# A graph network's gates and its experts in one stage: the gates computed in four groups, three of them between the experts' units

## The chip, the cores and the metric

The program runs on one core of one Trainium2 chip. Its metric is the device time of one execution in microseconds, the median of the runs. The profile was taken in one further execution.

## What is computed

The kernel is a tower of four layers over 16384 tokens of 64 features. The change touches the feed-forward part of the third layer: a graph attention gives every node four scores, the best two of them become gates, and a mixture of four experts, computed densely, is weighted by these gates.

```python
e = jax.nn.leaky_relu(a_src[src] + a_dst[dst], negative_slope=0.2)
e_max = jax.ops.segment_max(e, dst, num_segments=M)
ee = jnp.exp(e - e_max[dst])
denom = jax.ops.segment_sum(ee, dst, num_segments=M)
alpha = ee / (denom[dst] + 1e-16)
msg = h[src] * alpha[:, :, None]
agg = jax.ops.segment_sum(msg, dst, num_segments=M).reshape(M, HEADS * NUM_EXPERTS) + b_gat
scores = _layernorm(agg, ln_gamma, ln_beta).reshape(M, HEADS, NUM_EXPERTS).mean(1)
scores = scores.reshape(Bc, Nc, NUM_EXPERTS)
topk_s, topk_i = jax.lax.top_k(scores, TOP_K)
w = jax.nn.softmax(topk_s, axis=-1)
for ei in range(NUM_EXPERTS):
    g = jnp.where(topk_i == ei, w, 0.0).sum(-1)
    hh = jax.nn.gelu(x @ W1[ei] + b1[ei], approximate=False)
    out = out + g[..., None] * (hh @ W2[ei] + b2[ei])
```

## The kernel before

The program is a row of stages. Each is a `Stage` with its own tiles and semaphores, and ends with a barrier over all engines (L82). Inside a stage each engine has its own instruction stream, written out by hand, and semaphores tie the streams together, so the order of the work is the order of the code. Tokens lie in 128 tiles of 128 (`TILES`).

The third layer's feed-forward part (`ffn2`, L3941) has these stages around the change:

- `edge_softmax` runs over all edges and leaves in DRAM, row by row (`q.t_state`), the running softmax states of the edges sorted by destination.
- `carry_states` (L3753, names `carry_`) mends the states of nodes whose edges go over the end of a partition's row. It is a chain over SP, DVE, ACT and POOL, most of it on one partition, and ends with an indirect store by POOL (L3791).
- `node_gates` (L3841, names `gates_`): POOL issues 128 indirect gathers, one a tile (L3929), each 32 of them one group with a semaphore of its own. DVE waits for a group and merges it with the node's own state (L3880 to L3902), four times, 32 tiles at a time. Then it goes on over all 128 tiles at once: normalisation (L3905 to L3908), the scores (L3910, L3911), the best two in `top2_steps` (L665 to L685), and the gates split into three bf16 parts (`GateSplit.vector`, L775 to L779). PE turns them (L788) in 8 steps of 16 tiles, and ACT copies each step from PSUM into `g.GT` (L795). POOL, behind its gathers, clears the room for the split gates and makes the experts' tables (`ExpertTables`, L832 to L839); SP loads the weights (L817 to L828).
- `experts` (L1203, names `expc_`): 16 blocks of 8 tiles times 4 experts make 64 units. PE spreads a unit's gates over the partitions (`gate`, L1289, tile `gp`) and computes the first layer of the next unit (L1271, tile `hp`); ACT applies Gelu (L1351); DVE multiplies both into `hid` (L1394); PE multiplies by the second weights (L1303), with six bias matmuls at a block's first expert (L1301). At a block's end ACT copies the sum (L1341), PE turns it back (L1312, at the third unit of the next block), DVE adds it to `g.H` (L1372, one unit later) and takes the statistics of the block before (L1377).

Two rules of that loop matter here. PE's `gate(u)` waits until product u - 1 is done, since `gp` has one buffer. And PE's stream has for unit u the order gate(u), first layer (u + 1), second layer (u - 1).

## Time and profile before

| | |
|---|---|
| median of 3 runs | 6085.68 us (6083.33 to 6087.12) |
| the profiled execution | 6076.21 us, span 6074.5 us |
| PE busy | 4905.7 us (81%), mean granted clock 0.899 |
| DVE busy | 4695.5 us (77%) |
| POOL busy | 2671.5 us (44%) |
| ACT busy | 2461.6 us (41%) |
| from the first gather of `node_gates` to the last statistics of `experts` | 4611.3 to 4998.7 us of the span |

The granted clock stands in tenths or as a share: 1.00 is PE's full clock and 0.50 the half. Start times are microseconds from the span's start. PE is the matmul engine, PEld its weight loads, DVE the vector engine, ACT the scalar engine, POOL GpSimd, SP the engine that issues DMAs. A bracket behind a timeline row gives the engine's idle time just before and what ended it.

### The profile page before, as it was taken

What the parts mean: (1) busy time and instruction counts of PE and PEld (TensorE: products, weight loads), DVE (VectorE), ACT (ScalarE), POOL (GpSimd) and SP (SyncE); (2) the same over time, 40 slices, a digit from 0 to 9 for tenths busy, and PEclk for the clock granted to TensorE, in tenths of its full rate; (3) what the DMA queues carried; (4) which work ended last, traced back from release to release, by engine and by line L of the source; (5) the groups of instructions that cost most, each with busy time, mean ns of one, the idle gap of its engine ahead of it and who ended that gap; (6) DMA issues with size and microseconds to landing.
All of it is one profiled execution on the core that took longest, in us unless ns stands there. A gap on an engine that the chain in (4) does not pass through costs nothing. (4 is left out here: it accounts for less than half of the span.)

```text
span 6074.5 us, 108916 instructions
## 1 busy us (share of the span) xinstructions
PE 4905.7 (81%) x39862; PEld 3331.9 (55%) x39929; DVE 4695.5 (77%) x8591; ACT 2461.6 (41%) x4417; POOL 2671.5 (44%) x3019
## 2 busy tenths in 40 slices
PE   5567968886637999998799999999990298967998
PEld 3463226664424666665677777777770027852452
DVE  7896988897696888887588888888883467767657
ACT  4453433333434666666233333343340143222332
POOL 0000010000324675886667777777774301015557
PEclk8787989998668999999799999999995599978999
DMA  0300000111312110000122222222220000030252
GB/s 18 84 1 6 8 23 28 30 32 39 109 50 36 19 28 17 2 2 9 28 41 43 46 44 44 43 44 43 43 44 15 5 1 4 3 74 18 67 133 44
DMA packets 269133, 208.06 MB, mean 34 GB/s; under 512 B 139498, under 2 KB 242835, under 8 KB 267571
## 3 DMA queue, kind: packets, MB, share of 16 engines
q1 hardware_dynamic: 195806, 145.14, 8.5%
q0 software_dynamic: 72912, 57.02, 6.1%
q8 instruction: 269, 4.41, 0.3%
q14 instruction: 134, 1.10, 0.1%
q10 hardware_dynamic: 12, 0.39, 0.0%
HBM read 113.55 MB, written 69.40 MB: 30 GB/s over the span
## 5 line engine op out<-in xcount | busy, mean ns | idle before, releaser
L3514 PE MATMUL edges_bank<-part_room,hot_room 128*128 128x512 f32 x6656 | 1528.8, 391 | 78.2 <-ACT XT L3537 57.5
L3514 PEld LDWEIGHTS edges_bank<-part_room,hot_room 128*128 128x128 f32 x6656 | 1249.3, 188 | 357.8 <-ACT XT L3537 69.7
L3493 POOL DMA_INDIRECT XT<-gat_node_table,edges_idx x1216 | 1203.2, 989 | 392.5 <-issue 311.8
L3537 ACT COPY XT<-edges_bank 128x512 f32<-128x512 f32 x832 | 474.8, 597 | 657.6 <-PE edges_bank L3514 562.9
L3632 DVE COPY_PREDICATED XT<-edges_tabs_p,XT 128x1024 f32<-128x1024 int32 (+7 forms) x768 | 576.9, 751 | 38.3 <-DVE edges_acc_s L3681 7.1
L3613 DVE TENSOR_SCALAR hot_room<-edges_lanes,edges_nodes 128x512 fp32r<-128x512 f16 (+1 forms) x768 | 351.1, 518 | 172.0 <-PE edges_bank L3514 86.2
L505 POOL TENSOR_TENSOR X<-H,ln_f_mean 128x1024 f32<-128x1024 f32 x5 | 11.4, 2279 | 913.2 <-DVE ln_f_shift L542 913.2
L1837 ACT ACTIVATE GT<-attc_sc,attc_nm 128x256 f32<-128x256 f32 x1024 | 399.5, 480 | 32.0 <-DVE attc_nm L1915 32.0
L1915 DVE TENSOR_REDUCE attc_nm<-attc_sc 128x4 f32<-128x1024 f32 x256 | 312.8, 1222 | 110.1 <-PE attc_sc L1756 110.1
L1851 ACT ACTIVATE GT<-attc_sct 128x1024 f32<-128x1024 f32 x256 | 262.1, 1024 | 305.3 <-PE attc_sct L1767 305.2
L1756 PE MATMUL attc_sc<-XT,attc_tT 64*128 64x256 f32 x2048 | 296.5, 409 | 43.8 <-ACT GT L1837 43.8
L1920 DVE TENSOR_REDUCE attc_rs<-GT 128x4 f32<-128x1024 f32 x256 | 309.2, 1208 | 1.8 <-ACT GT L1837 1.8
L1777 PE MATMUL attc_op<-GT,attc_xB 128*64 128x256 f32 x2048 | 278.4, 392 | 5.2
L1767 PE MATMUL attc_sct<-attc_tT,XT 64*128 64x256 f32 x2048 | 268.3, 379 | 1.3 <-DMA attc_tT<-X 0.7
L1756 PEld LDWEIGHTS attc_sc<-XT,attc_tT 64*128 64x128 f32 x2048 | 185.8, 190 | 143.3 <-issue 117.2
L2190 ACT ACTIVATE X<-attb_r 128x2048 f32<-128x2048 f32 x64 | 120.1, 1877 | 270.3 <-PE attb_r L2147 270.3
L1767 PEld LDWEIGHTS attc_sct<-attc_tT,XT 64*128 64x128 f32 x2048 | 204.8, 188 | 21.4 <-ACT GT L1851 2.2
L788 PE MATMUL gates_gt<-identb,GT 128*128 128x128 bf16 x64 | 6.6, 277 | 259.9 <-DVE GT L779 258.5
L2486 DVE TENSOR_TENSOR X<-attd_r,attd_decay 128x2048 f32<-128x2048 f32 x64 | 146.6, 2291 | 81.8 <-PE attd_r L2389 81.7
L888 POOL DMA_INDIRECT sorted_in<-X,expd_in_slot x144 | 137.9, 958 | 145.6 <-SPq L1229 88.5
L1777 PEld LDWEIGHTS attc_op<-GT,attc_xB 128*64 128x64 f32 x2048 | 129.7, 136 | 126.7 <-issue 92.7
L2234 DVE TENSOR_REDUCE attb_mx<-attb_r 128x16 f32<-128x2048 f32 x64 | 146.3, 2287 | 65.0 <-PE attb_r L2133 65.0
(850 smaller groups left out, 10203.5 us busy)
## 6 DMA issues: line engine op xcount, KB each, us to landing
gat_states<-GT SPq DMA_DIRECT2D x32, 768.0 KB, 3.3
XT<-gat_node_table,edges_idx POOLq DMA_INDIRECT x1216
edges_lanes<-gat_places SPq DMA_DIRECT2D x128, 128.0 KB, 3.0
expert_pairs<-in_L_ffn_W_dram SPq DMA_DIRECT2D x48, 256.0 KB, 4.1
edges_lanes<-gat_places SPq DMA_DIRECT2D x64, 160.0 KB, 3.2
XT<-XT SPq DMA_DIRECT2D x32, 256.0 KB
XT<-XT SPq DMA_DIRECT2D x64, 128.0 KB
XT<-XT SPq DMA_DIRECT2D x128, 64.0 KB
```

Source lines behind the costliest of these rows:

```text
L1756: m = nc.tensor.matmul(sc[(0, 1, 1, 0)[hp]][:, n, a * S:(a + 1) * S], tT[half, b % NB, hp, a * P:(a + 1) * P], x(b, half), start=True, sto ...
L1767: m = nc.tensor.matmul(sct[:, n, j * S:(j + 1) * S], x(b, half)[:, j * P:(j + 1) * P], tT[half, b % NB, hp, :], start=True, stop=True)
L1777: m = nc.tensor.matmul(op[half, 0:S], xB[:, b % NB, j, (2 * hp + n) * D:(2 * hp + n + 1) * D], probT[:, hp % 2, n, j, :], start=hp + j == ...
L1837: m = nc.scalar.activation(prob[:, hp % 2, n, a, :], sc[(0, 1, 1, 0)[hp]][:, n, a * S:(a + 1) * S], ACT.Exp, bias=nm[:, b % 2, n, hp, a:a ...
L1851: nc.scalar.activation(probT[:, hp % 2].rearrange("p n j s -> p n (j s)"), sct[:], ACT.Exp).then_inc(probT_ready, 1)
L1915: vec.tensor_reduce(nm[:, b % 2, :, hp, :], sc[(0, 1, 1, 0)[hp]][:].rearrange("p n (a s) -> p n a s", s=S), AX.X, ALU.max, negate=True).th ...
L1920: vec.reduce_sum(rs[:, b % 2, :, hp, :], prob[:, hp % 2], AX.X).then_inc(totaled, 1)
L3493: nc.gpsimd.indirect_dma_start(out=rows[:, k, c, :], out_offset=None, in_=q.t_table, in_offset=bass.IndirectOffsetOnAxis(ap=idx[:, k, c:c ...
L3514: m = nc.tensor.matmul(banks[t][:], hot[:, (k * GROUPS + j) % 2, b, t, :], parts[:, p, b].rearrange("p u c -> p (u c)"), start=b == 0 and ...
L3537: nc.scalar.copy(fetched[:, (k * GROUPS + j) % 2, t].rearrange("p u c -> p (u c)"), banks[t][:]).then_inc(fetched_in, 1)
L3613: m = vec.tensor_scalar(hot[:, (k * GROUPS + j) % 2, b, 0:GROUP_SIZES[j]], lanes[:, j % LANE_SLOTS, 0:GROUP_SIZES[j]], nodes[:, b:b + 1], ...
L3632: vec.copy_predicated(half(0, w), taken(s, w), half(w, 2 * w)).then_inc(halved, 1)
```

## The change

`node_gates` and `experts` for this layer become one stage, `merged_experts`. The gates are computed wholly by groups of 32 tiles. The first group's gates come before the first unit. A group of 32 tiles is 16 units of the experts; in what follows w is a unit's place in its group, 0 to 15. The gates of the next group are cut into pieces that DVE runs behind the products of w = 6 to 11, ACT behind its Gelus of w = 7, 8 and 10, and PE turns them at w = 12 and 13, into the PSUM tile `yt`, which serves the turn-back too. The scale is an Exp of a Ln in place of a square root and a reciprocal. The loads of the expert tables (SP), the making of `pick` and `b2f` and the clearing of the gates' room (POOL) move to `carry_states`. The small tiles of the gates lie in the unused half of `g.XT`. Nothing of the computation is left out.

```diff
-def carry_states(nc, g, q):
+def carry_states(nc, g, q, tables):
...
                 sp.dma_start(carry[:], q.t_carry).then_inc(moved, 16)
+                tables.sync(sp)
...
+                tables.gpsimd(pool)
+                nc.gpsimd.memset(g.GT[:, TOKENS // 2:].bitcast(F32), 0.0).then_inc(gates_zeroed, 1)
+                pool.wait_ge(gates_zeroed, 1)
                 pool.wait_ge(merged_ready, 1)
...
-def node_gates(nc, g, q, b_gat, gamma, beta, ahead):
...
+def merged_experts(nc, g, q, b_gat, gamma, beta, tables):
...
+    GROUPS, GT = 4, TILES // 4
+    NB = TOKENS // (2 * U)
+    NU, PER = NB * E, NB * E // 4
...
+                for t in range(TILES):
+                    nc.gpsimd.indirect_dma_start(
+                        out=run[:, t, :], out_offset=None, in_=q.t_state,
+                        in_offset=bass.IndirectOffsetOnAxis(ap=q.end_row[:, t:t + 1], axis=0)).then_inc(gathered[t // GT], 16)
...
+                def turn_gates(c):
+                    pe.wait_ge(gates_split, c // 2 + 1)
+                    if c:
+                        pe.wait_ge(gates_moved, c)
+                    if c >= 2:
+                        pe.wait_ge(y_added, NB // GROUPS * (c // 2) - 2)
+                    for k in range(8):
+                        pair = g3[:, 16 * c + 2 * k:16 * c + 2 * k + 2, :].rearrange("p t c -> p (t c)")
+                        t = nc.tensor.transpose(yt[:].bitcast(BF16)[:, k * P:(k + 1) * P], pair, g.identb[:])
+                    t.then_inc(gates_turned, 1)
...
+                    if u % PER == 0:
+                        pe.wait_ge(gates_moved, 2 * (u // PER) + 2)
+                    if u:
+                        pe.wait_ge(hid_full, u)
...
+                def turn_back(i):
+                    pe.wait_ge(y_moved, i + 1)
+                    if i:
+                        pe.wait_ge(y_added, i)
+                    if i % 4 == 2 and i + 4 < NB:
+                        pe.wait_ge(gates_moved, 2 * (i // 4) + 4)
...
+                turn_gates(0)
+                turn_gates(1)
+                for u in range(NU):
+                    gate(u)
+                    if u + 1 < NU:
+                        first_layer(u + 1)
+                    if u:
+                        out(u - 1)
+                    if u % PER in (12, 13) and u // PER + 1 < GROUPS:
+                        turn_gates(2 * (u // PER) + u % PER - 10)
+                    if u % E == 2 and u > E:
+                        turn_back(u // E - 1)
+                out(NU - 1)
+                turn_back(NB - 1)
+
+            @block.scalar
...
+                def weights(n):
+                    act.wait_ge(diff_ready, n + 1)
+                    nc.scalar.activation(diff[:, n], diff[:, n], ACT.Exp).then_inc(exped, 1)
...
+                def scales(n):
+                    mine = mean[:, n * GT:(n + 1) * GT]
+                    act.wait_ge(var_ready, n + 1)
+                    nc.scalar.activation(mine, mine, ACT.Ln, bias=g.eps[:], scale=1.0 / CH).then_inc(logged, 1)
+                    act.wait_ge(logged, n + 1)
+                    nc.scalar.activation(mine, mine, ACT.Exp, scale=-0.5).then_inc(std_ready, 1)
...
+                def gaps(n):
+                    mine = second[:, n * GT:(n + 1) * GT]
+                    act.wait_ge(gap_ready, n + 1)
+                    nc.scalar.activation(other[:, n * GT:(n + 1) * GT], mine, ACT.Exp).then_inc(gap_exped, 1)
...
+                def move_gates(c):
+                    act.wait_ge(gates_turned, c + 1)
+                    nc.scalar.copy(g.GT[:, c * 8 * P:(c + 1) * 8 * P], yt[:].bitcast(BF16)).then_inc(gates_moved, 1)
...
+                    act.wait_ge(hp_full, u + 1)
+                    if u >= 2:
+                        act.wait_ge(hid_full, u - 1)
+                    nc.scalar.activation(act_out[:, u % 2], hp[u % 2][:], ACT.Gelu, bias=b1s[:, e:e + 1]).then_inc(act_done, 1)
+                    if n + 1 < GROUPS:
+                        if w == 7:
+                            weights(n + 1)
+                        if w == 8:
+                            scales(n + 1)
+                        if w == 10:
+                            gaps(n + 1)
+                    if e == 0 and i:
+                        move_y(i - 1)
+                    if n + 1 < GROUPS and w in (13, 14):
...
+                def normed(n):
...
+                    v.wait_ge(std_ready, n + 1)
+                    link(vec.tensor_tensor(num[:, s], num[:, s], bc(mean[:, s], 2, CH), ALU.mult))
+                    link(vec.tensor_tensor(num[:, s], num[:, s], bc(params[:, 1], 1, GT), ALU.mult))
+                    link(vec.tensor_tensor(num[:, s], num[:, s], bc(params[:, 2], 1, GT), ALU.add))
+                    link(vec.reduce_sum(L[:, s], num[:, s].rearrange("p t (h e) -> p t e h", h=HEADS2), AX.X))
+                    link(vec.tensor_scalar(L[:, s], L[:, s], 1.0 / HEADS2, None, ALU.mult))
...
+                def one_hot(best, s):
+                    link(vec.tensor_reduce(best[:, s], L[:, s], AX.X, ALU.max))
+                    link(vec.tensor_tensor(hot[:, s], L[:, s], bc(best[:, s], 2, E), ALU.is_equal))
+                    link(vec.tensor_tensor(tmp[:, s], hot[:, s], bc(rev, 1, GT), ALU.mult))
+                    link(vec.tensor_reduce(r[:, s], tmp[:, s], AX.X, ALU.max))
+                    link(vec.tensor_tensor(hot[:, s], bc(rev, 1, GT), bc(r[:, s], 2, E), ALU.is_equal))
...
+                def piece(n, w):
+                    if w == 6:
+                        merge(n)
+                    if w == 7:
+                        shares(n)
+                        values(n)
+                        centre(n)
+                        spread(n)
+                    if w == 8:
+                        normed(n)
+                        best_of(n)
+                    if w == 9:
+                        second_of(n)
+                    if w == 10:
+                        mix(n)
+                    if w == 11:
+                        split(n)
...
+                for w in range(PER):
+                    piece(0, w)
+                for u in range(NU):
+                    i, e = divmod(u, E)
+                    n, w = divmod(u, PER)
+                    v.wait_ge(act_done, u + 1)
+                    v.wait_ge(gp_full, u + 1)
+                    if u >= 2:
+                        v.wait_ge(hid_used, u - 1)
+                    vec.tensor_tensor(hid[:, u % 2], act_out[:, u % 2], gp[:], ALU.mult).then_inc(hid_full, 1)
+                    if e == 3 and i:
+                        add(i - 1)
+                    if n + 1 < GROUPS:
+                        piece(n + 1, w)
+                    if e == 0 and i >= 2:
...
-            carry_states(nc, g, q)
-            node_gates(nc, g, q, I["L2_ffn_b_gat"], I["L2_ffn_ln_gamma"], I["L2_ffn_ln_beta"], ahead=tables)
-        experts(nc, g, "expc", tables, target=g.H, measure=True)
+            carry_states(nc, g, q, tables)
+            merged_experts(nc, g, q, I["L2_ffn_b_gat"], I["L2_ffn_ln_gamma"], I["L2_ffn_ln_beta"], tables)
```

DVE, around the products of w = 7 and 8 of the first group (L4169 is the product, L4039 to L4071 the merge and what follows it, L4140 the addition to `g.H`). Before, no such rows stood between products; now these do:

```order
+L4039 TENSOR_TENSOR XT<-X,XT 128x128
+L4040 TENSOR_TENSOR XT<-X,XT 128x128
+L4041 TENSOR_TENSOR XT<-XT 128x128
+L4169 TENSOR_TENSOR expc_hid<-expc_act_out,expc_gp 128x1024
+L4140 TENSOR_TENSOR H<-H,expc_yt 128x512
+L4046 TENSOR_TENSOR XT<-XT,X 128x128
+L4047 TENSOR_TENSOR XT<-XT 128x128
+L4048 TENSOR_SCALAR XT<-XT 128x128
+L4049 RECIPROCAL XT<-XT 128x128
+L4050 TENSOR_TENSOR XT<-XT 128x256
+L4057 TENSOR_TENSOR X<-X,XT 128x32x4 x4
+L4057 TENSOR_TENSOR X<-gat_table,XT 128x32x4 x4
```

The merge of the next group now stands ahead of product w = 7, and the longest piece between the products of w = 7 and 8.

ACT, from the Gelu of w = 8 to that of w = 11 (L4017 is the Gelu, L3987 the Ln, L3989 and L3994 the Exps, L4004 the copy of the block's sum):

```order
+L4017 ACT_TABLE_LOAD
+L4017 ACTIVATE expc_act_out<-expc_hp,expc_in_b 128x1024
+L3987 ACT_TABLE_LOAD
+L3987 ACTIVATE XT<-XT,eps 128x32
+L3989 ACT_TABLE_LOAD
+L3989 ACTIVATE XT<-XT 128x32
+L4004 COPY expc_yT<-expc_yp 128x512
+L4017 ACT_TABLE_LOAD
+L4017 ACTIVATE expc_act_out<-expc_hp,expc_in_b 128x1024 x2
+L3994 ACT_TABLE_LOAD
+L3994 ACTIVATE XT<-XT 128x32
+L4017 ACT_TABLE_LOAD
```

Where there was one table load in front of 64 Gelus, ACT now changes its table seven times in each of three groups.

POOL, in `carry_states` and behind it:

```order
+L3789 DMA carry_first<-gat_states,gat_first_end 128x24
 L832 MEMSET expc_in_pick 128x256
 L834 MEMSET expc_in_b2f 128x64
 L839 AFFINE_SELECT expc_in_pick<-expc_in_pick 128x512 x6
...
+L3791 MEMSET GT 128x4096
+L3795 DMA gat_states<-carry_merged,gat_first_end 262145x24
```

The tables and the clearing stood behind the 128 gathers and now stand between the two indirect DMAs of `carry_states`.

## Rows read from the trace of the kernel before

**Rows 1.** The page, part 1: busy time, share of the span and instructions of each engine.
```profile
PE 4905.7 (81%) x39862; PEld 3331.9 (55%) x39929; DVE 4695.5 (77%) x8591; ACT 2461.6 (41%) x4417; POOL 2671.5 (44%) x3019
```

**Rows 2.** Busy time by stretch: window, PE, PEld, DVE, ACT, POOL, clock, DMA share, GB/s.
```profile
4611.00:4653.00 42.00, 0.00 (x0) 0.00 (x0) 1.42 (x4) 0.00 (x0) 31.65 (x34) 0.50 0.14 20
4653.00:4774.00 121.00, 0.00 (x0) 0.00 (x0) 26.87 (x69) 1.25 (x3) 92.35 (x97) 0.50 0.10 10
4774.00:4815.00 41.00, 0.29 (x3) 0.29 (x4) 37.92 (x53) 3.69 (x5) 6.51 (x9) 0.50 0.00 0
...
4826.00:4999.00 173.00, 167.16 (x800) 49.80 (x800) 104.13 (x208) 78.70 (x81) 0.00 (x0) 0.97 0.00 1
```

**Rows 3.** Timeline, POOL (start, length, engine, line, operation, idle before).
```profile
4611.29 0.96 POOL L3929 DMA_INDIRECT X<-gat_states,gat_end_row  x1 [3.01 <-POOLq L82]
...
4771.61 0.94 POOL L3929 DMA_INDIRECT X<-gat_states,gat_end_row  x1 [0.30 <-issue]
```

**Rows 4.** Timeline, DVE, the first group's pieces.
```profile
4652.58 0.29 DVE L3880 TENSOR_TENSOR gates_m<-X,gates_own_e 128x128 f32<-128x128 f32 x1 [40.51 <-DMA X<-gat_states,gat_end_row]
...
4653.89 0.29 DVE L3885 TENSOR_TENSOR gates_den<-gates_diff,X 128x128 f32<-128x128 f32 x1 [0.48 <-ACT gates_diff L3920]
...
4656.24 0.93 DVE L3894 TENSOR_TENSOR X<-X,gates_diff 128x128 f32<-128x128 f32 x4
...
4661.90 0.69 DVE L3902 TENSOR_REDUCE gates_mean<-X 128x32 f32<-128x512 f32 x1
```

**Rows 5.** Timeline, DVE, the piece over all 128 tiles, and the first product.
```profile
4794.73 3.78 DVE L3910 TENSOR_REDUCE gates_L<-X 128x512 f32<-128x2048 f32 x1
...
4814.22 0.43 DVE L779 CAST GT<-XT 128x512 bf16<-128x512 f32 x1
...
4829.82 1.22 DVE L1394 TENSOR_TENSOR expc_hid<-expc_act_out,expc_gp 128x1024 f32<-128x1024 f32 x1 [4.00 <-ACT expc_act_out L1351]
```

**Rows 6.** Timeline, ACT, table loads and gate copies.
```profile
4775.27 1.28 ACT L3922 ACT_TABLE_LOAD   x1
...
4815.78 1.93 ACT L795 COPY GT<-gates_gt 128x1024 bf16<-128x1024 bf16 x2 [7.72 <-PE gates_gt L788]
...
4827.38 1.28 ACT L1351 ACT_TABLE_LOAD   x1 [3.56 <-PE expc_hp L1271]
```

**Rows 7.** Timeline, PE, gate matmuls at the full clock, four units apart and one apart.
```profile
4904.48 0.39 PE L1289 MATMUL expc_gp<-GT,expc_in_pick 64*128 64x512 bf16 x2
...
4912.48 0.39 PE L1289 MATMUL expc_gp<-GT,expc_in_pick 64*128 64x512 bf16 x2
...
4914.67 0.39 PE L1289 MATMUL expc_gp<-GT,expc_in_pick 64*128 64x512 bf16 x2
```

**Rows 8.** Timeline, DVE, the stage's last instructions.
```profile
4996.58 2.12 DVE L1377 BATCH_NORM_STATS2 stats<-H 128x6 f32<-128x64 f32 x16
```

**Rows 9.** Timeline, PE, one unit at the half clock, and the gate matmul of the next.
```profile
4831.10 0.61 PE L1289 MATMUL expc_gp<-GT,expc_in_pick 64*128 64x512 bf16 x2 [1.67 <-DVE expc_hid L1394]
...
4833.35 1.49 PE L1301 MATMUL expc_yp<-GT,expc_b2p 64*64 64x512 bf16 x6
4834.77 1.97 PE L1303 MATMUL expc_yp<-expc_hid,expc_in_w 128*64 128x512 f32 x4
4836.67 0.54 PE L1289 MATMUL expc_gp<-GT,expc_in_pick 64*128 64x512 bf16 x2
```

**Rows 10.** Busy time by stretch, columns as in rows 2, where the clock moves.
```profile
4824.00:4826.00 2.00, 0.03 (x2) 0.06 (x2) 1.04 (x5) 0.00 (x0) 0.00 (x0) 1.00 0.00 0
4828.00:4836.00 8.00, 6.33 (x20) 1.30 (x16) 2.44 (x2) 3.90 (x4) 0.00 (x0) 0.50 0.00 0
4836.00:4838.00 2.00, 2.00 (x9) 0.52 (x7) 0.69 (x1) 0.00 (x0) 0.00 (x0) 0.75 0.00 0
```

**Rows 11.** Timeline, DVE beside POOL's affine selects, and the selects.
```profile
4778.40 1.65 DVE L3894 TENSOR_TENSOR X<-X,gates_diff 128x128 f32<-128x128 f32 x4
...
4776.68 4.71 POOL L839 TENSOR_SCALAR_AFFINE_SELECT expc_in_pick<-expc_in_pick 128x512 bf16<-128x512 bf16 x6 [0.16 <-POOL expc_in_b2f L834]
```

More of the change, by code:

```diff
@@ new lines, in merged_experts @@
+        at = 2 * TILES * HEADS2
+        own_e, m, den = (spare[:, at + k * TILES * HEADS2:at + (k + 1) * TILES * HEADS2].rearrange("p (t h) -> p t h", h=HEADS2)
+                         for k in range(3))
+        at += 3 * TILES * HEADS2
+        L, G, hot, tmp = (spare[:, at + k * TILES * E:at + (k + 1) * TILES * E].rearrange("p (t e) -> p t e", e=E) for k in range(4))
+        at += 4 * TILES * E
+        mean, first, second, r, share, other = (spare[:, at + k * TILES:at + (k + 1) * TILES] for k in range(6))
@@ L3873, in _, with merge @@
                 link = chain(v, own)
-                link(vec.tensor_tensor(own_e[:], q.table[:, :, CH:TAB], q.a_dst[:], ALU.add))
-                link(leaky(vec, own_e[:], own_e[:]))
-                v.wait_ge(loaded, 48)
-                for n in range(GROUPS):
+                def merge(n):
                     s = slice(n * GT, (n + 1) * GT)
@@ L3912, in _ @@
-                steps, parts["pool"], parts["act"] = top2_steps(nc, v, link, st, L[:], G[:], E, hot[:], tmp[:])
-                steps()
-                gates.vector(v, link, G[:])
-            @block.scalar
-            def _(act):
-                for n in range(GROUPS):
-                    act.wait_ge(diff_ready, n + 1)
-                    nc.scalar.activation(diff[:, n], diff[:, n], ACT.Exp).then_inc(exped, 1)
-                act.wait_ge(var_ready, 1)
-                nc.scalar.activation(mean[:], mean[:], ACT.Sqrt, bias=g.eps[:], scale=1.0 / CH).then_inc(std_ready, 1)
-                parts["act"](act)
-                gates.scalar(act)
@@ L3926, in _ @@
-            @block.gpsimd
-            def _(pool):
-                for t in range(TILES):
-                    nc.gpsimd.indirect_dma_start(
-                        out=run[:, t, :], out_offset=None, in_=q.t_state,
-                        in_offset=bass.IndirectOffsetOnAxis(ap=q.end_row[:, t:t + 1], axis=0)).then_inc(gathered[t // GT], 16)
-                parts["pool"](pool)
-                gates.gpsimd()
-                ahead.gpsimd(pool)
-            @block.tensor
-            def _(pe):
-                gates.tensor(pe)
+                    vec.reduce_sum(mean[:, s], part[:, s], AX.X).then_inc(var_ready, 1)
@@ new lines, in add, with moments @@
+                def add(i):
+                    v.wait_ge(y_turned, i + 1)
+                    h = target[:, 8 * i:8 * i + 8, :].rearrange("p t d -> p (t d)")
+                    vec.tensor_tensor(h, h, yt[:], ALU.add).then_inc(y_added, 1)
+                def moments(i):
+                    v.wait_ge(y_added, i + 1)
+                    for t in range(8 * i, 8 * i + 8):
+                        mm = vec.bn_stats(g.stats[:, t, :], target[:, t, :])
+                    return mm
+                v.wait_ge(tables.loaded, 16 * tables.LOADS)
```

159 lines of the change are left out of this document (132 added, 27 removed).

## The prediction

> **What bounds the kernel now.** I read the page first, then a table of stretches, then the timelines of the engines inside them. On the page no engine is busy all the time, PE being the first with 81% [rows 1], so what counts is which wait ends last in the stages that the change touches. The stretches [rows 2] show two halves that never overlap. From 4611 to 4774 us PE does nothing and DVE is busy 28 of 163 us: this is POOL's row of 128 gathers, 4611.29 to 4771.61 by their starts, one each 1.26 us [rows 3]; DVE's idle time in front of the first merge is put down to them [rows 4]. From 4774 to 4815 DVE is full and PE idle, and from 4826 PE is busy 167 of 173 us, DVE 104. So first the gathers bound, then DVE, then PE. The change lays the gathers of three groups, and their share of DVE's work, beside the experts.
>
> How the clock behaves bears on the price. PE's granted clock was still 1.00 in a stretch in which it did next to nothing, then 0.50 from 4828 to 4836, although PE was busy for most of it, and rose again inside the next 2 us [rows 10]. So here PE fell to the half clock (1.2 of 2.4 GHz) behind an idle stretch, and was back at the full one after 8 us with 6.3 of work.
>
> **The new start of the experts.** The first group's merge can start where it did, at 4652.58, when its 32 gathers have landed, and the old code then runs unchanged to the end of L3902 at 4662.59, 10.0 us [rows 4]. Next on ACT a Ln, a table load and an Exp: 1.28 for the load [rows 6], two ACTIVATEs on 32 columns at some 0.3 and the handshakes, 2.2 us. Then normalisation and scores for 32 tiles: three operations on 512 columns and a copy-like one on 128, 3 x 0.73 + 0.26, and the strided reduction, a quarter of 3.78 [rows 5], in all 3.4. The two searches for the best are ten operations on 128 columns at about 0.33 with the gap (0.29 for one [rows 4]) and three small ones: 2.2 + 1.85. The mix is 1.75 with its reciprocal on 32 columns, the split 1.35, the exponential between them 0.4. Sum 10.95, call it 10.9: the gates of 32 tiles are split at 4652.58 + 10.0 + 2.2 + 10.9 = 4675.7. Two turns by PE at the half clock and two copies by ACT (1.93 for two [rows 6]) alternate on one bank: 4.4, so 4680.1. The Gelu's table load and one Gelu, 1.28 + 1.1, put the first product at 4682.5, against 4829.82 before [rows 5]. **That is 147.3 us earlier.** From the first product to the last statistics it was 4829.82 to 4998.70, 168.9 us [rows 5, 8]; without further cost the stage would end 147.3 us earlier. The b2 parts and the node's own terms run while DVE waits for the gathers: nothing, and one barrier with its start-up is inside the 147.3 already.
>
> **The cost behind the experts.** At the full clock a unit takes 2.19 us, a block of four 10.19 with its bias matmuls and turn-back [rows 7]. DVE needs 1.22 of it for the product [rows 5], so has about one microsecond free. The pieces of one group are 0.86 for the merge, 8.7 for w = 7 (4653.89 to 4662.59 [rows 4]), 5.6 for w = 8 (3.4 + 2.2), 1.85, 1.75 and 1.35: 20.1 us in six units. They can't be hidden in six free microseconds; and since gate(u + 1) waits for product u while the next product waits for the piece, nothing is caught up later. I step through it, t = 0 at the end of product 6:
> - product 7 runs 0.9 to 2.1 behind the merge, then 0.7 for the addition and 8.7: t = 11.5. The Exp between has its load done beside it.
> - product 8 to 12.7. ACT's Ln, load and Exp end at 13.4, DVE does 3.4 + 2.2, then 1.1 of statistics: t = 20.1.
> - product 9 to 21.3, its piece to 23.2. PE has idled most of 17 us and is at the half clock: gate, first layer and second layer of a unit then take 4.15 (5.57 with 1.42 of bias [rows 9]) instead of 2.19. So product 10 ends at 24.4, but PE finishes the unit at 29.6, with the turn-back and the return of the clock at about 28.
> - product 11 to 27.6; the addition behind it waits for that turn-back until 29.6, the split ends at 31.7, product 12 at 32.9.
> - the two turns of the gates cost PE 0.4 each and gate(14) comes at 36.4, gate(15) at 39.2.
> Without pieces gate(15) comes at 20.4, counting 10.19 a block. **Each of the three groups loses 18.8 us, call it 19, together 57.** Gathers don't join this path: group two must be there at product 6, about 17 us after 4682.5, so 4700, and landed at 4693 by the old pace (64 times 1.26 behind 4611.3, and the landing); for the later ones the room is more than 20 us.
>
> How low and high can the 57 be? With PE at the full clock throughout, the same steps give 16 a group, 48. If PE instead stays at the half clock from w = 9 to the end of each group, gate(13), (14) and (15) come at 36.0, 42.4 and 47.8: 27.5 a group, 82.
>
> **The carry stage.** POOL's six affine selects take 4.71 us, and DVE's four small operations beside them 1.65 where 0.93 is usual [rows 11, 4]. Now they lie beside the start of DVE's chain in `carry_states`, which is on the path: at the least nothing, since the chain has other forms; at the most they stretch it over their whole length, 4.7 x 0.44 = 2.1, and the clearing as much again, 4. I take 2.5, nearest to the selects' own ratio. POOL itself is done long before the merged rows are. SP's ten issues come behind the last load of the chain, beside DVE's work and the store.
>
> **The sum.** 147.3 - 57 - 2.5 = 87.8 us less. The profiled execution had 6076.21 us, which gives 5988.4; it lay 9.5 below the median of the runs, and against that median of 6085.68 the forecast is **5998 us**.
>
> ACT's table changes are the place where a page and the rows differ. In the rows a load takes 1.28 us and the next ACTIVATE follows at once [rows 6]; with that only the load between Ln and Exp is on the path. The Trainium skill (ScalarE: Activation LUTs, What ACT_TABLE_LOAD costs) gives a drain of about 1.38 us on top, some 2.66 for each switch. With two of a group's seven switches on the path, an estimate by that page adds about 3 us a group, and the forecast would be some 6006 us.
>
> **The rivals.**
> 1. The clock stays up in the pieces, since PE still does a unit's work now and then: 48 in place of 57, so 5989. For it speaks that the clock fell only some microseconds after the idle time began [rows 10]; against it that the pieces of w = 7 and 8 hold PE up for two long waits.
> 2. The clock falls and comes back late, at each group's end: 82 in place of 57, so 6023. PE in w = 9 to 12 still has short waits for products, which speaks for it; that before it rose within 10 us of the start, with such a wait in between, speaks against.
> 3. The other side, slower than before: **PE never gets out of the half clock in this stage**, because every group brings a new break. Then a block takes 4 x 4.15 + 1.42 + 1.2 = 19.2, 9.0 more than 10.19; 16 blocks make 144, the two long pieces another 11 in each of three groups, 33, less about 4 of the same that was there at the start before. 147.3 - 144 - 33 + 4 - 2.5 = -28: 6114 us. It decides the sign once the units lose more than 144.8 / 64 = 2.3 us each on average. Against it speaks that four blocks of a group hold ten units without any piece. The Trainium skill (TensorE: Matmul & The Clock Gate, Part 1 and HAM oscillation) says that the half rate is the default, that activity releases it, and that a kernel whose PE waits again and again can fall back at each wait. By that rule the clock falls anew in each group, as I assumed; only if it never rose between would this rival hold.
> 4. The overlap doesn't come off: gathers slowed by DVE's work, or the first units waiting for the second group. With the gathers binding throughout, the last group can't be merged before 4774, and behind it lie 20.1 of pieces, 4.4 of turns, the last 16 units, 41, and some 9 of the last block's end: 4849, well before my end at 4911. So the gathers would have to slow by some 60 us in 160; DVE's merges in the old trace lie beside gathers that keep their 0.94.
>
> **How the numbers follow.** My forecast with its own unknowns (the small operations' durations, the carry stage, the table loads) has a chance of 0.55; rival 1 0.15, rival 2 0.2, rival 3 0.03, rival 4 or a mishap of its kind 0.07. The forecast's own range is 5988 to 6010; taking in rivals 1 and 2 and the bound of 4 us for the carry stage it is 5980 to 6028. About 0.2% (12 us) is what a measurement of this kernel can tell from no change. All cases but the third, and part of the fourth, are faster by far more: faster 0.95, same 0.015, slower 0.035.
>
> **What would show it.** In the profile after, the first product should start near 4682, the last statistics end near 4911. In DVE's timeline the pieces should lie in clusters of about 31 us between products 6 and 12 of three groups, and PE's waits should name the product, L4169, for some 50 us in all. The last group's blocks should keep 10.2 us. The granted clock should fall once in each of three groups. I am wrong if the first product is later than 4695, if the last group's units are slower than before, if an ACT load appears as the releaser in front of several products, or if DVE waits for gathers inside the experts.

## The result, and the profile after

| | before | after |
|---|---|---|
| median of the runs, us | 6084.51 (6072.29 to 6087.12) | 5977.19 (5975.13 to 5981.42) |
| profiled execution, us | 6076.21 | 5975.13 |
| its span, us | 6074.5 | 5973.4 |
| first product, us | 4829.82 | 4677.81 |
| last statistics end, us | 4998.70 | 4895.34 |

The ratio is 0.984, 95% interval 0.9818 to 0.9861: faster by 107.3 us, where 87.8 were forecast. 5977 lies 3 us below the range that I gave.

The two profiled executions differ by 101.1 us, but not all of that is in code that the change touches. I measure the touched stretch from SP's last store of edge states, the last thing ahead of `carry_states`, to the last statistics: before 4576.26 to 4998.70, **422.4 us**; after 4567.72 to 4895.34, **327.6 us**. That is 94.8 less. The store itself stands 8.5 us earlier, behind code that is the same, and what follows is 2.3 us longer. So the change is worth about 95 us, and the forecast missed it by 7.

The page, part 1, of the kernel after, beside [rows 1]: PE's share goes from 81 to 83%, DVE's from 77 to 79%, over a span that is 101 us shorter.

```profile
PE 4928.8 (83%) x39929; PEld 3337.0 (56%) x39929; DVE 4706.3 (79%) x8677; ACT 2491.8 (42%) x4448; POOL 2671.6 (45%) x3019
```

Timelines of POOL, DVE and DVE (start, length, engine, line, operation, idle before): the first gather, the first merge, the first product, and the last rows of the stage.

```profile
4606.25 0.98 POOL L3898 DMA_INDIRECT X<-gat_states,gat_end_row  x1 [0.56 <-issue]
...
4647.85 0.36 DVE L4039 TENSOR_TENSOR XT<-X,XT 128x128 f32<-128x128 f32 x1 [39.78 <-DMA X<-gat_states,gat_end_row]
...
4677.81 1.22 DVE L4169 TENSOR_TENSOR expc_hid<-expc_act_out,expc_gp 128x1024 f32<-128x1024 f32 x1 [6.81 <-ACT expc_act_out L4017]
...
4893.22 2.12 DVE L4145 BATCH_NORM_STATS2 stats<-H 128x6 f32<-128x64 f32 x16
```

First merge to first product is 29.96 us; the forecast had 29.9. From the first gather to the first product it is 71.6 us where it was 218.5 [rows 3, 5]. Then comes the price. DVE's timeline of the first cluster, rows left out between:

```profile
4693.90 1.22 DVE L4169 TENSOR_TENSOR expc_hid<-expc_act_out,expc_gp 128x1024 f32<-128x1024 f32 x1 [0.55 <-PE expc_gp L3934]
...
4696.68 1.22 DVE L4169 TENSOR_TENSOR expc_hid<-expc_act_out,expc_gp 128x1024 f32<-128x1024 f32 x1 [0.82 <-PE expc_gp L3934]
4697.82 0.68 DVE L4140 TENSOR_TENSOR H<-H,expc_yt 128x512 f32<-128x512 f32 x1
4698.42 0.28 DVE L4046 TENSOR_TENSOR XT<-XT,X 128x128 f32<-128x128 f32 x1
...
4706.44 0.69 DVE L4071 TENSOR_REDUCE XT<-X 128x32 f32<-128x512 f32 x1
4707.04 1.21 DVE L4169 TENSOR_TENSOR expc_hid<-expc_act_out,expc_gp 128x1024 f32<-128x1024 f32 x1
...
4715.95 1.20 DVE L4169 TENSOR_TENSOR expc_hid<-expc_act_out,expc_gp 128x1024 f32<-128x1024 f32 x1
...
4722.13 1.22 DVE L4169 TENSOR_TENSOR expc_hid<-expc_act_out,expc_gp 128x1024 f32<-128x1024 f32 x1 [0.42 <-PE expc_gp L3934]
```

Product 8 follows product 7 by 10.4 us and product 9 follows by 8.9, where 2.2 is a unit's usual time. The waits of the stage (engine, who waits for whom: total us, times, longest) name the product where I said they would, though 35.8 and not some 50 us:

```profile
PE expc_gp L3934 <- DVE expc_hid L4169: 35.8, 7, 7.7
...
ACT XT L3987 <- DVE XT L4071: 17.4, 3, 5.9
...
DVE X L4076 <- ACT XT L3989: 2.4, 3, 0.8
```

DVE waited for ACT's results 0.8 us in each group; ACT waited for DVE. The clock fell in each of the three groups, and twice in each, where the forecast had one fall. Stretches of the first group, then three of the second (columns as in rows 2, the clock third from the right):

```profile
4700.00:4704.00 4.00, 0.64 (x4) 0.00 (x0) 3.86 (x12) 1.28 (x1) 3.09 (x4) 0.92 0.10 9
4704.00:4708.00 4.00, 0.00 (x0) 0.00 (x0) 3.83 (x7) 0.83 (x2) 3.13 (x3) 0.50 0.09 9
4708.00:4712.00 4.00, 3.69 (x14) 1.05 (x14) 3.10 (x5) 3.96 (x6) 3.35 (x3) 0.50 0.10 9
4712.00:4716.00 4.00, 1.85 (x6) 0.26 (x4) 3.69 (x18) 2.21 (x2) 2.84 (x4) 0.80 0.07 9
4716.00:4720.00 4.00, 2.79 (x8) 0.94 (x10) 3.83 (x10) 1.08 (x2) 3.02 (x4) 0.63 0.10 9
4720.00:4724.00 4.00, 4.00 (x22) 1.28 (x20) 3.41 (x10) 2.67 (x3) 3.09 (x4) 0.94 0.11 10
4724.00:4728.00 4.00, 4.00 (x28) 1.43 (x26) 3.62 (x15) 1.98 (x3) 3.09 (x4) 1.00 0.11 13
...
4764.00:4768.00 4.00, 2.87 (x10) 1.01 (x12) 3.13 (x4) 3.94 (x6) 3.09 (x4) 0.50 0.09 9
4768.00:4772.00 4.00, 1.63 (x10) 0.20 (x4) 3.66 (x13) 3.03 (x3) 1.06 (x2) 0.93 0.05 6
4772.00:4776.00 4.00, 2.06 (x6) 0.65 (x6) 3.83 (x15) 0.34 (x2) 0.00 (x0) 0.50 0.02 4
```

As the clock has two levels, the shares from 4700 to 4724 add up to 13.7 us at the half one in the first group.

The gathers went on under all this: the last one starts at about 4768, and no group waited for them.

### The profile page after: what moved, and what is told of

Its sections match the earlier page's. It is cut to its first block and busy times, and to the rows that moved or that the text cites. A ratio compares the mean times of both kernels' runs of the same rounds, so it can differ in the third digit from the quotient of the medians.

```text
span 5973.4 us, 109087 instructions
## 1 busy us (share of the span) xinstructions
PE 4928.8 (83%) x39929; PEld 3337.0 (56%) x39929; DVE 4706.3 (79%) x8677; ACT 2491.8 (42%) x4448; POOL 2671.6 (45%) x3019
## 5 line engine op out<-in xcount | busy, mean ns | idle before, releaser
L1351 ACT ACTIVATE expa_act_out<-expa_hp,expa_in_b 128x1024 f32<-128x1024 f32 x128 | 141.0, 1115 | 133.6 <-PE expa_hp L1271 133.5
```

## The experiments

My theory: the price of the overlap is DVE's work beyond what a unit leaves free, because gate(u + 1) needs product u and there is one bank `gp`, so nothing is caught up. The rivals were the half clock, ACT's table loads, and the gathers. "Length" below is always first product to end of the last statistics: 168.9 before, 217.5 after. Experiments 1 to 8 are one execution each, on several chips, so I compare lengths and not whole times; the three kernels that were profiled twice repeat their length within 0.7 us.

**1. No pieces behind the experts.**
```
-                    pe.wait_ge(gates_split, c // 2 + 1)
+                    pe.wait_ge(gates_split, 1)
-                        piece(n + 1, w)
+                    if n + 1 < GROUPS and w == 6: v.wait_ge(gathered[n + 1], 16 * GT)
-   (ACT) weights(n + 1), scales(n + 1), gaps(n + 1)
```
The gates of the second, third and fourth group are not computed; waits for gathers, turns and copies stay.

> Left out: the gates of the second, third and fourth group (their pieces on DVE and ACT; those gates stay zero); the gathers, the turns by PE and the copies by ACT stay. In the changed kernel the stretch from the first product to the last statistics is 217.5 us, against 168.9 before. Theory (DVE's pieces hold up the products): it comes back to 168 to 172 us, the two turns of the gates costing at most 1 us a group, and the clock stays at 1.00 from some 8 us after the first product. Rival (the turns through the shared bank, or the gathers beside the experts, cost something themselves): 175 us or more.

Measured: length 171.1 us, 5940.64 us (before on that chip 6080.58). The groups take 42.5, 41.8 and 41.8 us from first product to first product, where after has 57.6, 57.3 and 57.6. So the pieces cost 15.1, 15.5 and 15.8, together 46.4, and the turns, copies and gathers beside them 2.2. PE is busy throughout a group:

```profile
4734.00:4776.00 42.00, 41.98 (x222) 13.28 (x222) 26.11 (x53) 21.48 (x23) 31.90 (x34) 1.00 0.11 11
```

The gathers as a bound (rival 4 of the prediction) fall.

**2. No table changes.** Ln and Exp become Identity at four places, so the gates' values are others while the instructions keep their shapes.
```
-nc.scalar.activation(diff[:, n], diff[:, n], ACT.Exp)
+nc.scalar.activation(diff[:, n], diff[:, n], ACT.Identity)
...
```


> The Exp and Ln of the gates are replaced by Identity, so that ACT changes its table no more behind the first Gelu; values change, all instructions on DVE and PE stay. Theory (DVE's pieces bind, of ACT's switches only the one between Ln and Exp and a wait or two are on the path): 217.5 us shrinks by 2 to 6, about 1.3 a group plus the first group's. Rival (ACT's table loads bind the products, 7 times 1.28 a group): it shrinks by 15 to 27 us.

Measured: length 215.7, 1.8 us less for 21 changes; groups 58.3, 55.7 and 56.7, so the first is even 0.7 longer. Ahead of the first product another 1.3 us are gone. ACT's table loads as a cause fall; even my 2 to 6 was slightly too much.

**3. Tables and clearing out of the carry stage**, behind the first 32 gathers, which changes the carry stage alone ahead of the gathers.
```
 (carry_states)  -tables.gpsimd(pool); memset(g.GT[...])   -tables.sync(sp)
 (POOL, gathers) +if t == GT - 1: tables.gpsimd(pool); memset(g.GT[...])
```


> The making of the tables and the clearing of the gates' room leave carry_states and come behind the first 32 gathers of the merged stage; the b2 parts are made after the first group's merge. Theory (the selects and the clearing beside DVE's chain in carry_states cost the 3.5 us by which the first gather came later): from the last store of the states (SP) to the first gather it is 35.0 us as before the change instead of 38.5; the later groups' gathers come some 9 us later, the second group's merge then waits up to 4 us, so that the whole gains 0 to 3 us. Rival (the 3.5 us come from SP's ten loads or the longer wait at the barrier): the 38.5 us shrink by less than 1, or only by what SP's part explains.

Measured: last store to first gather 34.96 us, against 35.03 before and 38.53 after; the touched stretch 324.8, 2.8 less than after. So the carry stage paid 3.5 us, as the theory had it. DVE's rows there, in after and then in this run:

```profile
4576.69 0.68 DVE L3338 TENSOR_SCALAR carry_reset<-carry_cont 1x128 f32<-1x128 f32 x1
4577.41 2.71 DVE L3340 TENSOR_TENSOR_SCAN X<-carry_reset,X 1x128 f32<-1x128 f32 x4
4581.53 1.21 DVE L3345 TENSOR_SCALAR carry_diff<-carry_diff 1x512 f32<-1x512 f32 x1
```
```profile
4580.85 0.21 DVE L3338 TENSOR_SCALAR carry_reset<-carry_cont 1x128 f32<-1x128 f32 x1
4581.10 1.87 DVE L3340 TENSOR_TENSOR_SCAN X<-carry_reset,X 1x128 f32<-1x128 f32 x4
4584.39 0.41 DVE L3345 TENSOR_SCALAR carry_diff<-carry_diff 1x512 f32<-1x512 f32 x1
```
The three rows take 2.5 us with POOL idle beside them and 4.6 with its selects and memset there. From its first comparison of the row ends to the end of L3345 DVE takes 4.9 us here and before, 7.9 in after: 3.0 of the 3.5. The rest is POOL's own store (L3795 in after), issued 0.8 us behind the merged rows in place of 0.3. SP's ten loads left the stage in the same run, so the edit alone doesn't clear them; but in after they start at 4597.52, behind all the longer rows, and no DVE row behind them is longer than here.

**4. Hold the clock.** PE turns the identity onto itself in the two long waits.
```
+                    if n + 1 < GROUPS and w in (9, 10):
+                        pe.wait_ge(y_added, 4 * n + 1)
+                        for _ in range((40, 30)[w - 9]):
+                            nc.tensor.transpose(yt[:, 0:P], g.ident[:], g.ident[:])
```


> The kernel of the change, in which TensorE turns the identity matrix onto itself 40 times ahead of the gate matmuls of w = 9 and 30 times ahead of those of w = 10, in the three groups that have pieces, where it stood idle for 7.7 and 3.4 us. The transposes go into the bank that holds the turned sum, after VectorE has read it, and nothing reads them. Theory (the half clock that follows the long pieces costs next to nothing, because VectorE's pieces of w = 8 and 9 are the longer chain while it lasts, and only the units of w = 10 and 11 still run into TensorE at the slow clock): the granted clock stays at 1.00 through all three groups, and each group is 0.3 to 1.0 us shorter, the stretch from the first product to the last statistics 214.5 to 217 us long against 217.5. Rival (the half clock is what the short-falling pieces cost: 9 us a group were set down for it in the prediction's dearer case against the case in which it stays up): 205 us or less. Second rival (the transposes themselves hold up the gate matmuls behind them): 219 us or more, with TensorE's wait for the product gone and its transposes still running when the product ends.

Measured: length 215.3, 2.3 less, inside the theory's 214.5 to 217; groups 57.6, 56.3, 56.3. The clock didn't stay up throughout, as the theory had it. In the first group it dipped behind the second lot (0.64) and nothing was gained; in the third it stood at 1.00 through the first long piece and fell within the second (0.87 and 0.70, some 3.4 us at the half level where the first group of after has 13.7):

```profile
4802.00:4806.00 4.00, 4.00 (x24) 1.40 (x24) 3.14 (x7) 3.88 (x4) 0.00 (x0) 1.00 0.00 0
4806.00:4810.00 4.00, 4.00 (x29) 2.43 (x26) 3.79 (x14) 2.61 (x3) 0.00 (x0) 1.00 0.00 0
...
4814.00:4818.00 4.00, 2.33 (x12) 0.83 (x12) 3.13 (x5) 3.52 (x5) 0.00 (x0) 0.87 0.01 4
4818.00:4822.00 4.00, 4.00 (x22) 2.07 (x21) 3.69 (x10) 3.47 (x4) 0.00 (x0) 0.70 0.00 0
```

So taking most of the half clock away gives 1.0 to 1.3 us in the second and third group. The expectation's "9 us a group" misreads my own prediction, which had 2.8 between the forecast and the case in which the clock stays up (18.8 and 16), and 11.5 for the dearer case (27.5); both are too much. It costs little at w = 8, where DVE's piece and the statistics take from 4709.05 to the next product at 4715.95 while PE's unit, at 1.2 GHz, ends at 4713.9. Behind the short piece of w = 9 PE is the longer one: product 11 waits 0.42 us for it (the row of 4722.13 above).

**5. Small parts, spread.** The six pieces become 17 parts, placed by the free time of each unit, from unit 5, 17 and 32 up to the unit w = 11; each ACT operation follows one unit behind.
```
+        FREE = (1.28, 0.63, 1.64, 0.4)          # DVE's free us behind product e = 0..3
+        starts = {1: 5, 2: 17, 3: 32}
-                        piece(n + 1, w)
+                    for group, name in plan.get(u, ()): step(group, name)
```


> The same work for the gates, cut into 17 parts and spread over more units: the second group's over units 5 to 11, the third's over 17 to 27, the fourth's over 32 to 43, as early as the gathers allow. Theory (DVE's work is hidden only as far as each unit has free time, 15.7 us in 16 units): 48.6 us of cost fall to about 31 (13.6 + 9.2 + 8.3), so 217.5 becomes 200, and 14 to 19 us less in all; the clock no longer falls in the third and fourth group. Rival (the half clock is the cost, not DVE's time): the third and fourth group lose nearly nothing, and 217.5 becomes 187 or less. Rival (ACT's switches): no change within 5 us.

Measured: length 203.0, 14.5 less than after; groups 56.3, 50.9, 50.8. I had forecast 200. What the theory gives, worked out once the run was known: a group has 20.5 us of parts; free in units 5 to 11 are 6.6, in 17 to 27 10.6, in 32 to 43 11.9. The excess is 13.9 + 9.9 + 8.6 = 32.4, and 171.1 + 32.4 = 203.5. Against the groups of experiment 1 the three pay 13.7, 9.1 and 9.1. The first group, with seven units in place of six, gained only 1.3 us of the 14.5, so most of the gain comes from more units and not from smaller parts. The clock still fell once in the third group (half from about 4817 to 4820), against the forecast.

**6. Statistics deferred, tables early.** On top of 5: the statistics of blocks 0 to 11 go into the last 20 units, the tables into the normalisation ahead of the attention.
```
+                    if u >= NU - 20 and done < 96:
+                        some = min(QUOTA[e], 96 - done); moments(done, some); done += some
+        turned_norm(nc, g, "ln_f2", g.H, known=True, ahead=tables)
```


> The version with small parts spread over the units, with two further changes. First, the statistics of the first twelve blocks leave the groups that have pieces and go into the last group, where VectorE has about 4 us free in each block of 10.2; so each unit w = 0, 4, 8, 12 of the first three groups has 1.1 us more room for gates. Second, the tables' selects (POOL) and loads (SP) leave the carry stage for the normalisation ahead of the attention, where POOL stands idle behind its last product; only the clearing of the gates' transposes stays in the carry stage. Theory: VectorE's own work bounds the first three groups, so taking 12 x 1.1 = 13 us of it away shortens the stretch from the first product to the last statistics from 203.0 to 188 to 193 us, with the last group still at 10.2 us per block; the first gather comes 34.5 to 36.5 us after the last store of states instead of 38.6; together 12 to 19 us less than the spread version. Rival (order of the parts, not the amount of VectorE's work, sets the length: waits for the turns and for TensorE's gate matmuls behind each product): 198 us or more. Second rival (the statistics are only moved, and the last group grows by what the others lose): last group 11 us per block or more, and the sum within 3 us of 203. If the tables' move costs what it gives, the normalisation's stage ends 2 us or more later.

Measured: length 203.6, groups 58.4, 50.6, 49.6, the last 45.0 to its last statistics, as in all the versions of 32 tiles. My theory's 188 to 193 was wrong, and the length lies on the first rival's side. I had subtracted 12.7 us, and less than that left: of the 80 statistics that stood in the first three groups 30 still do, in units 44 to 47, so DVE was relieved of some 6.9 us there. Six of the relieved units also hold parts, which makes 6.6 us of relief where it should count, and that gave nothing either. The lump that I blamed first doesn't explain it: products 6 and 7 start 6.8 us apart, with some 5.6 us of steps between them, but they did so in experiment 5 too. Two things that the trace shows took something back: DVE's wait for the scale (4.4 us in all, 2.4 in 5), and unit 44, which takes 3.5 us with 16 statistics in it, in place of 2.2. The rest stays open. The first gather came 36.9 us behind the store, 1.6 sooner.

**7. Single steps.** 49 steps in place of 17 parts, with no room carried over; the fourth group's begin at unit 30.
```
+            for u in range(first_unit, 16 * n - 4):
+                spent = 0.0
+                while k < len(STEPS) and spent + STEPS[k][0] / 2 <= FREE[u % E] + over: ...
```


> The version before (statistics moved into the last group, tables early), with the 17 parts of a group's gates cut into 49 single steps. Each unit takes steps for as much time as VectorE has free in it (2.4, 0.6, 1.6 and 0.4 us for the four experts of a block) and an equal excess, and room that a unit leaves is not carried over to the next; so the lumps go (6.9 us of steps between products 6 and 7, 8.4 us between products 9 and 10 with a wait for the scale in them). Theory (a unit takes the longer of TensorE's work and VectorE's, and time that VectorE has free in one unit cannot be used in another): the excess over the free time, by the table of steps, is 13.6, 7.8 and 6.3 us in the three groups, so they take 55, 49.5 and 48 us against 58.4, 50.6 and 49.6, and the stretch from the first product to the last statistics 195 to 200 us against 203.6. TensorE's clock stays at 1.00 from the second group on. Rival (short steps lose by the waits between them and by ScalarE's table loads, which now fall beside the Gelus one by one): 203 us or more.

Measured: length 202.9; groups 57.9, 51.1, 48.9. The forecast of 195 to 200 failed. The excess by the table of steps is 27.7, which gives 198.8. DVE's wait for the scale, whose chain of Ln, Exp and two loads has only one short unit to hide in, is 4.2 us:

```profile
DVE X L4101 <- ACT XT L4022: 4.2, 3, 2.0
```

Its size is that of the miss, but it was 4.4 us in experiment 6 and 2.4 in experiment 5, where the sum came out without it. So it explains at most 1.8 of the 4.1 us, and the rest stays open. The two ways to spread end alike, 203.0 and 202.9, though DVE has some 6.9 us less to do in the first three groups here. Counting the excess unit by unit fits experiment 5; what it promised for relieving DVE came in neither 6 nor 7. The first group stays the dearest in both: seven units lie between its gathers and its turn.

**8. Eight groups of 16 tiles.** On top of 7, with two tiles' statistics per unit. The first product waits for 16 gathers, and each group's gathers are there before its units.
```
-    GROUPS, GT = 4, TILES // 4
+    GROUPS, GT = 8, TILES // 8
-                    if u % PER in (12, 13) and u // PER + 1 < GROUPS:
+                    if u % PER == 5 and u // PER + 1 < GROUPS:
```


> The version with single steps, and eight groups of 16 tiles in place of four of 32: the first product then waits for 16 gathers in place of 32, one group's steps run beside the eight units before its own, and two tiles' statistics stand in each unit. Theory: the first group's gates start 20 us earlier and take 5 to 7 us less on half the tiles, so the first product comes 44 to 48 us after the first gather in place of 71.5. A step on half the tiles takes more than half its time, 14.3 us in all against 20.5 by the sizes seen, so VectorE's excess is some 6 us a group: seven groups at 25 to 28 us and the last at 20, the stretch from the first product to the last statistics 205 to 217 us. From the first gather to the last statistics that makes 250 to 264 us, against 275.1 in the version before and 289.0 in the kernel of the change. Rival (ScalarE becomes the bound: three changes of the table out of and back into Gelu in each group are 9 us of loads beside 11 us of work, in a group of 25 us): groups of 30 us or more, DVE's products waiting for ScalarE's Gelus, and from the first gather to the last statistics 275 us or more.

Measured: first gather 4609.85, first product 4653.50, 43.65 behind it; length 224.3; first gather to last statistics 267.9, against 289.1 in after. The first product came as forecast, the length 7 us and the whole 4 us over it. The length itself is 21 us more than in experiment 7; the gain is the first product, 28.0 us sooner. Two stretches of this kernel, two groups each:

```profile
4714.00:4771.00 57.00, 42.74 (x218) 13.18 (x216) 51.58 (x157) 41.25 (x44) 43.20 (x46) 1.00 0.11 11
4771.00:4827.00 56.00, 42.29 (x218) 13.17 (x216) 50.50 (x157) 41.25 (x44) 0.00 (x0) 1.00 0.01 1
```

DVE is busy 90% of the time and PE 75%: the bound has moved to DVE, whose steps on 16 tiles take more than half of those on 32 (13.3 us busy in the second group, 18.8 in after). ACT, at 73%, is not the bound. PE at that share kept the full clock.

**9. Timing, five rounds on one chip,** beside nine runs of the kernel before (median 6063.67, 6057.41 to 6074.88).

The kernel of the change: 

> The kernel of the change itself, timed in rounds beside the kernel before. Between the two profiled executions the stretch from the last store of states to the last statistics was 94.8 us shorter and the rest, whose code is the same, 6 us. Theory (only the touched stretch changes): 90 to 100 us less than the kernel before on this chip too, a ratio of 0.9835 to 0.985. Rival (the changed program also gains in code that it does not touch): 103 us or more.

Small parts: 

> The version with 17 small parts spread over the units, timed in rounds. From the touched stretch (327.6 in the kernel of the change, 313.2 here): 12 to 17 us less than the kernel of the change on the same chip.

Eight groups: 

> The version with eight groups of 16 tiles and single steps, timed in rounds. From the touched stretch (304.7 us here): 20 to 26 us less than the kernel of the change on the same chip, and 6 to 11 us less than the version with small parts. If the tables that were moved into the normalisation cost time there, less.

| | median, us | ratio to before, 95% | touched stretch, us |
|---|---|---|---|
| after | 5970.89 (5968.65 to 5973.98) | 0.9845 (0.9831 to 0.9858) | 327.5 |
| small parts | 5966.05 (5951.19 to 5978.49) | 0.9832 (0.9815 to 0.9848) | 313.1 |
| eight groups | 5954.25 (5951.62 to 5957.37) | 0.9818 (0.9805 to 0.9832) | 305.5 |

After is 92.8 us faster than before here, as the theory and the touched stretch have it; the further 14 us between the medians of the first measurement don't repeat. The touched stretches repeat within 0.8 us. The medians of the two further versions gain less than their stretches: 4.8 for 14.4, and 16.6 for 22.0. So both of my forecasts for the whole failed, 12 to 17 and 20 to 26, and eight groups are 11.8 ahead of small parts, not 6 to 11. The five executions of small parts alone span 27 us, those of the other two 5 and 6. In the profiled executions the last store stands at 4565.26 (after) and 4588.21 (small parts). The attention's edge stage ahead of it takes 1617 us in both, so the 23 us arise before it, in code that is the same. Of them 16.6 arise in the program's first stage, where PE is the busy engine: the next stage's first load is issued at 117.67 in after and at 134.26 in small parts (and at 134.22 in the profile of experiment 7, whose whole time of 5981.81 us, against 6073.40 of the kernel before on its chip, is no better than after's). PE's matmuls there, from 45 to 60 us, in this experiment's profiles of after and then of small parts (busy us, mean ns, idle before):

```profile
L281 PE MATMUL embed_spread_p<-X,embed_sel 6*128 6x512 bf16 x24 | 6.2, 376 | 0.0
```
```profile
L281 PE MATMUL embed_spread_p<-X,embed_sel 6*128 6x512 bf16 x12 | 5.6, 622 | 0.0
```

From 90 to 110 us both take 376 or 377 ns, and the granted clock in 60 to 90 is 1.00 in after and 0.83 in small parts. So the clock came up later there, and fell once more; why is not shown.

Eight groups are faster than the change: the ratios' intervals overlap by a ten-thousandth, the executions themselves not at all. For the small parts the timing alone doesn't tell.

## Why the prediction was right, and where it was off

- **The mechanism held.** First product near 4682: it came at 4677.8, and counted from the last store, which stood 8.5 earlier, 143.5 us sooner than before against a forecast of 147.3 - 2.5 = 144.8. The carry stage makes 1.0 of the difference: 3.5 us, not 2.5.
- **Length.** Forecast 168.9 + 57, measured 217.5: 48.7 more. This is the term that was mis-sized, 8.3 us too dear.
- **Its steps.** Counted from the end of product 6 of the first group (4695.12), forecast and measured: product 7 ends 2.1, 2.8; product 8 12.7, 13.1; product 9 21.3, 22.0; product 10 24.4, 24.9; product 11 27.6, 28.2; product 12 32.9, 31.3; gate(14) 36.4, 34.8; gate(15) 39.2, 37.6. Up to product 11 all is 0.4 to 0.7 late. The step that failed is "PE finishes the unit at 29.6, with the turn-back and the return of the clock at about 28": the turn-back ended at 26.5. The clock had come up at about 4714 and fallen again by 4717 (0.80, then 0.63 above), so PE began its work behind product 9 at the half clock, as I had it (0.61 us for two gate matmuls). But it was up again early in 4720 to 4724 (0.94), by that share some 25.4 us behind product 6 and not 28. PE's rows, from the two long waits to the turn-back:

```profile
4708.31 0.61 PE L3934 MATMUL expc_gp<-GT,expc_in_pick 64*128 64x512 bf16 x2 [7.67 <-DVE expc_hid L4169]
...
4717.21 0.61 PE L3934 MATMUL expc_gp<-GT,expc_in_pick 64*128 64x512 bf16 x2 [3.35 <-DVE expc_hid L4169]
...
4720.94 0.65 PE L3957 MATMUL expc_yt<-ident,expc_yT 128*128 128x128 f32 x4
```

  That is 1.6 us a group. Another 1.0 a group is in the yardstick: I counted gate(15) at 20.4 without pieces by an even 10.19 a block, but from product 6 on it is 21.4, since the turn-back falls into that part of a block. So 16.2 in the first group and 16.6 in the second, where I had 18.8.
- **Rival 1 (48 for a clock that stays up)** gave nearly the measured number for the wrong reason, and its nearness is luck. The clock did fall, twice in each group. Experiment 4 shows that holding most of it up is worth 2.3 us in all, where I had put 9 between the two cases.
- **Rivals 2 and 3** (clock back late, or never): it was at 0.94 in 4720 to 4724 and 1.00 after; the last group's blocks took 10.18 us. The Trainium skill's rule (TensorE: Matmul & The Clock Gate, HAM oscillation) that an engine which waits again and again can fall back at each wait agrees with two falls in each of three groups, one in each of the two long waits; but in experiment 5 eight waits of up to 2.9 us in the second group left the clock at 1.00.
- **ACT's table changes.** The rows of after show a load ahead of its operation, and the operation directly behind it:

```profile
4707.16 0.32 ACT L3987 ACTIVATE XT<-XT,eps 128x32 f32<-128x32 f32 x1 [5.87 <-DVE XT L4071]
4707.50 1.28 ACT L3989 ACT_TABLE_LOAD   x1
4708.79 0.23 ACT L3989 ACTIVATE XT<-XT 128x32 f32<-128x32 f32 x1
```

  Of the 1.38 us of drain that the Trainium skill (ScalarE: Activation LUTs, What ACT_TABLE_LOAD costs) adds to a load, no row here shows anything. The gap on either side of the load is 0.01 to 0.02 us, and experiment 2 gained 1.8 us in all from 21 fewer changes. The extra 3 us a group, estimated from that page, did not come.
- **The total.** The saving was 107.3 by medians for 87.8 forecast. Of those 19.5 us 7.0 are the terms above, 6.2 are code that is the same (8.5 - 2.3), and 6.2 come from where the profiled executions lie among their runs. In experiment 9 the saving was 92.8, 5 us from the forecast. My range had no room for that scatter below.

## What to carry to other kernels

When a stage's work is laid behind another engine's, price it unit by unit: each unit takes the longer of the two engines' work, and free time in a unit that holds nothing of the moved work is lost. Then ask how many units lie between the arrival of the inputs and the deadline: using more of them gave 14.5 us here. Smaller groups gave 22 us in another way, by an earlier first unit, and paid part of it back, since the moved work on half the data takes more than half the time. Taking work off the same engine elsewhere gave nothing measurable, which the counting by units did not foresee. Measure such a change over its own stretch as well as over the whole, since code ahead of it can move by more than the gain (23 us against 14 here, most of it by when the clock came up at the program's start).

## What the runs showed of the hardware that I had not expected

- Operations of DVE on a single partition slow down beside POOL's selects and memset too, but not all of them: TENSOR_SCALAR on 1x512 took 1.21 us beside POOL's memset in place of 0.41, on 1x128 0.68 beside the selects in place of 0.21. TENSOR_TENSOR on 1x127 took 0.70 beside the selects in place of 0.28, but on 1x512 beside the memset 0.68 as without it. In the trace of before the wide ones had gone from 0.93 to 1.65 [rows 4, 11].
- A transpose of 128x128 onto itself took 0.12 us of PE in experiment 4 (24.3 us for 210), less than I had allowed, so 40 of them filled only some 4.6 of the 7.7 us.
- The clock at the program's start came up at different times in kernels whose code there is the same: the same matmul took 376 ns in one and 622 in the other at 45 to 60 us, and the stage ended 16.6 us later (experiment 9).
